# Attention and feed-forward block on one core: the V products moved ahead of the group's piece in TensorE's order

## What is computed

```python
xn = layernorm(x)
# attention branch, 16 heads of 16 features
u, v, q, k = split(silu(xn @ W1 + b1), 4)          # W1: 256 x 1024
scores = einsum("bqhd,bkhd->bhqk", q, k)           # 1024 x 1024 per head
av = einsum("bhqk,bkhd->bqhd", silu(scores) / S, v)
y_attn = layernorm(av * u, gamma, beta) @ W2 + b2
# feed-forward branch, ternary weights, 256 -> 1024 -> 256
h = gelu(layernorm(xn, ln1) @ ternary(w1).T + fb1)
y_ffn = layernorm(h, ln2) @ ternary(w2).T + fb2
out = x + y_attn + y_ffn
```

## Time and profile before

| what | value |
|---|---|
| median of 3 runs | 1671.26 us |
| lowest, highest | 1669.81, 1671.69 us |
| span of the profiled execution | 1672.0 us, first to last instruction; no time beside it is recorded |
| granted TensorE clock, mean | 0.992 of full |
| PE busy | 1575.4 us |
| PEld busy | 762.4 us |
| ACT busy | 1235.2 us |
| DVE busy | 967.6 us |

### The profile page before, as it was taken

The page is one execution under the profiler, slowest core; times in us unless marked ns, Lnnn a source line. Parts: engine busy times, 40 slices in busy tenths (PEclk is TensorE's granted clock), DMA queues, the critical chain, the costliest instruction groups (busy, mean ns, idle before and its releaser), DMA issues.

```text
span 1672.0 us, 27962 instructions
## 1 busy us (share of the span) xinstructions
PE 1575.4 (94%) x9660; PEld 762.4 (46%) x9826; DVE 967.6 (58%) x1844; ACT 1235.2 (74%) x1285; POOL 101.7 (6%) x193
## 2 busy tenths in 40 slices
PE   4799999999999999999999999999999999999997
PEld 3344445444454444444445444544445444454433
DVE  5475645766366563665646655475645756356543
ACT  2477876788668886678767787677876788767884
POOL 2000100001000100001000010000100001000000
PEclk9899999999999999999999999999999999999999
DMA  6470034600445015530345303461034600345000
GB/s 183 97 150 28 1 77 117 135 26 17 89 113 112 26 36 104 120 80 19 75 92 124 67 1 76 92 151 36 1 76 113 141 26 16 84 114 116 1 1 26
DMA packets 110459, 123.68 MB, mean 74 GB/s; under 512 B 6640, under 2 KB 106608, under 8 KB 109296
## 3 DMA queue, kind: packets, MB, share of 16 engines
q1 hardware_dynamic: 110320, 121.81, 32.1%
HBM read 79.84 MB, written 41.94 MB: 73 GB/s over the span
## 4 chain that ended last, share of the span: by engine, by line
PE 70%; ACT 11%; issue 7%; DMA 5%; DVE 3%; SPq 1%; DVEq 0%; ACTq 0%; POOL 0%; POOLq 0%
PE scores L899 22%; PE outs L918 21%; ACT attn L531 9%; PE fill L955 7%; PE fill L989 7%; PE fill L973 5%; DMA QS<-q_scratch 4%; PE fill L982 2%; PE fill L964 2%; PE fill L1005 2%; DMA q_scratch<-qst 1%; PE fill L945 1%; DVE tmp L789 1%; ACT L531 1%; ACT L575 1%
## 5 line engine op out<-in xcount | busy, mean ns | idle before, releaser
L531 ACT ACTIVATE attn<-scores 128x1024 f32<-128x1024 f32 x1024 | 992.2, 1022 | 355.8 <-PE scores L899 353.5
L899 PE MATMUL scores<-QS,KS 128*128 128x512 bf16 x1882 | 514.9, 384 | 62.0 <-issue 28.2
L918 PE MATMUL outs<-attn,V 128*32 128x512 f32 x4096 | 548.7, 608 | 0.4 <-ACT attn L531 0.4
L899 PEld LDWEIGHTS scores<-QS,KS 128*128 128x128 bf16 x2048 | 148.4, 97 | 609.6 <-ACT attn L531 410.1
L789 DVE TENSOR_TENSOR tmp<-fill,l2g 128x512 f32<-128x512 f32 x128 | 88.6, 692 | 147.6 <-PE fill L982 142.0
L918 PEld LDWEIGHTS outs<-attn,V 128*32 128x32 f32 x4096 | 80.8, 108 | 150.4 <-issue 138.3
L989 PE MATMUL fill<-Wq,hgh 128*128 128x256 f32 x512 | 135.6, 303 | 0.3 <-DVE tmp L789 0.2
L955 PE MATMUL fill<-xp,W1h 128*128 128x512 f32 x384 | 132.1, 425 | 3.0 <-DVE xp L813 3.0
L772 DVE SCALAR_TENSOR_TENSOR hid<-fill,ratq,fb1b 128x512 f32<-128x512 f32 x128 | 96.1, 751 | 51.1 <-PE fill L973 39.9
L989 PE MATMUL fill<-Wq,hgl 128*128 128x256 f32 x512 | 125.0, 282 | 0.0
L800 DVE SCALAR_TENSOR_TENSOR part<-fill,cq,part 128x256 f32<-128x256 f32 x64 | 31.0, 484 | 129.6 <-PE fill L989 128.4
(11 more groups left out here) (113 smaller groups left out, 1462.4 us busy)
## 6 DMA issues: line engine op xcount, KB each, us to landing
KS<-k_scratch SPq DMA_DIRECT2D x64, 384.0 KB, 7.1
QS<-q_scratch SPq DMA_DIRECT2D x64, 384.0 KB, 8.3
k_scratch<-kst SPq DMA_DIRECT2D x160, 128.0 KB
q_scratch<-qst SPq DMA_DIRECT2D x96, 128.0 KB
xin<-in_x SPq DMA_DIRECT2D x8, 1024.0 KB, 4.8
KS<-k_scratch SPq DMA_DIRECT2D x32, 256.0 KB, 10.1
QS<-q_scratch SPq DMA_DIRECT2D x32, 256.0 KB, 10.6
out_dram<-part SPq DMA_DIRECT2D x16, 512.0 KB, 2.7
```

The source lines that it names most:

```text
L531: nc.scalar.activation(attn[:, g % 2, 2 * hf:2 * hf + 2, :], SP[:, 2 * hf:2 * hf + 2, :], ACT.Silu).then_inc(s_silu, 1)
L899: ins = mm(SP[:, j, :], KS[:, head, t * P:(t + 1) * P], QS[:, head, h * HALF:(h + 1) * HALF], start=True, stop=True)
L918: ins = mm(OP[32 * j:32 * j + 32, g // RUN % 2, :], V[:, t, c * HPC // 2 + j, o * DH:o * DH + 2 * DH], attn[:, g % 2, j, :], start=(o == 0 ...
```

## The change

In `body` of TensorE the V products of group g-1 move from behind the pieces of group g (and behind the setup products of the first batch) to directly behind the scores of group g. Group 0 and all other engines are as they were.

```diff
                     scores(b, g, first)
                     if g == 0 and not first:
                         times_v(b - 1, GROUPS - 1, False)
+                    if g:
+                        times_v(b, g - 1, first)
                     if first:
                         setup_step(g)
                     for s in steps(g, first, last):
                         step(b, *s)
-                    if g:
-                        times_v(b, g - 1, first)
```

## The result

The changed kernel takes 1713.5 us (median of 4 runs, 1712.6 to 1714.8) against 1671.5 us for the kernel before in the same comparison: ratio 1.0249, 95% interval [1.0236, 1.0263]. The forecast was 1708 us with a range of 1697 to 1724. The profiled span grew from 1672.0 to 1713.0 us, by 41.0 us where the sum said 36.5.

The account below looks back on a forecast made before the run. TensorE's own order was taken to bound groups with a piece. Exposed loads 27.7, gelu.0 5.9 and key and query halves 2.9 us summed to 36.5 us on 1671.3: 1708 us, range 1697 to 1724.

Parts of the forecast that it names:

- the 410 us of "wait for SiLU": Scores' weight loads, 541 waits: of each idle time 0.84 us is the V products running; only what exceeds it is waiting.
- The exposed load: Piece's first load, uncovered behind the V products: 0.093 us in 237 fp32r groups, 0.043 in 132 transpose groups; 27.7 us.
- with nothing lost: Joint from piece to next scores: in group 0 the scores follow the last transpose without loss.
- gelu.0: Group 15: VectorE empties f1.1.1 later, so gelu and group 17's scores come 0.73 us later, 8 times; 5.9 us.
- some 1.3: Predicted sign: a wait for SiLU of some 1.3 us between group 16's piece and group 17's scores.
- The key and query halves: Group 4's scores wait for the DMA restacking q.0.1 of group 61: 0.58 us more, 5 times; 2.9 us.
- pause at the loop's turn: At two of seven batch starts, a pause said to cover group 4's wait for the restacked halves.
- Projections and `xt`: ScalarE's steps for projections and transposed inputs end later but delay nothing that shows; 0 us.
- the rival that all held steps show: ScalarE's held steps cost 0.16 us on each of 96 projections: 15 us more, 1723 us; chance 0.09.
- A hidden load: Rival: the piece's load hides under the V products; only the two uncovered places cost, 11.6 us, 1683 us; chance 0.10.
- Pieces that stop waiting for VectorE: Rival, faster: a piece starting 1 us later finds its input ready; at most 10 us gained, 1662 us; chance 0.04.
- 10 / 369: The faster rival decides only if an exposed load costs less than this, given as 0.026 us.

Follow-up runs that it names:

- the experiment with the fourth score: Against the kernel before, in groups with an fp32r piece: three scores, V products, fourth score, piece; old order elsewhere; 1693.1 us, ratio 1.0120.
- 29 pairs: Kernel before with V products of two neighbouring groups run as one block at 29 places; 1665.5 us, ratio 0.9960; repeated: 1667.4 us, 0.9963.

## Why the prediction was right

**What bounds the kernel.** The reading held that the 410 us of "wait for SiLU" were mostly the V products' own running. The new page shows it: half the wait vanished, its 0.84 us reappeared in front of the pieces, and empty groups didn't change by 0.01 us.

**The exposed load, 27.7 us forecast, 31 measured.** Right in kind, place and sign for both kinds of piece, and the experiment with the fourth score shows the cause. The term was mis-sized for fp32r: 0.093 us forecast, 0.105 measured, 237 times. The difference is the bf16 load of the scores at the piece's other end. The prediction took "with nothing lost" from a row where the scores follow transposes. Behind an fp32r product the scores' load isn't drawn under it, so the bf16 load is exposed after all: 0.105 is close to the full 0.108 of an fp32r load, and the 0.015 that was subtracted isn't saved. The transposes, where the row did apply, came out at 0.046 for 0.043.

**gelu.0, 5.9 us forecast, 6.3 measured.** Right, in all eight batches, and undone by one group's order. Groups 15 and 16 together grew by 0.99 us where 0.92 was forecast. The idle time between group 16's piece and group 17's scores is 1.64 us where "some 1.3" was forecast; about 0.27 of it is the joint behind an fp32r product, as at the end of group 7.

**The key and query halves, 2.9 us forecast, 2.9 left over.** The agreement is luck in the main. Above its own load, group 3 with the wait for these halves grew at all seven starts and not five, by 4.1 us in all. The "pause at the loop's turn" that was to cover it at two of them was TensorE at half its granted clock for a stretch in that one execution. Without the two stretches 3.2 us are gone, one in batch 7 costs 1.5, and the other differences at the starts fill the rest. The chain hangs on `k.0.1` as well as on `q.0.1`; both were moved by the same 1.09 us. How much of the 4.1 us is the change's is uncertain. The first run with 29 pairs has the old order at these starts, and its group 3 grew by 1.2 and 0.7 us in batches 2 and 5 as well, where its clock doesn't fall; at the other starts it differs from before by up to 0.8 us either way.

**Projections and `xt`, 0 forecast.** Right for the projections: 12 in a batch show nothing but their load. For `xt` it was 0.06 us in groups 45 and 57, 0.8 us in all; in the kernel that moves only the fp32r groups, and so not `xt.1`, group 45 is unchanged. ScalarE's held step does delay a SiLU there; the rival that all held steps show is thereby as good as excluded for groups of 2.4 us and longer.

**The rivals.** A hidden load would have left groups with pieces unchanged; they all grew. Pieces that stop waiting for VectorE would have shown as shorter groups at the start of batches or at 42 and 43; apart from group 0 of batches 2 and 5, which is the clock, there is only group 63, and that differs by up to 0.7 us from before in kernels with the old order as well. The bound of that rival, 10 / 369, is 0.027 us and not 0.026, which changes nothing.

The Trainium skill's page "TensorE: Matmul & The Clock Gate", section "Step-by-step: what each phase is for", has loads pulled ahead of running products. The rows of after agree inside the pieces, behind transposes and behind bf16 scores, and disagree at two joints: a full-array load behind V products (0.84 us idle) and a bf16 load behind an fp32r product (0.28 us idle).

## What to carry to other kernels

Before a wait is blamed on the engine that the table names, compare its idle time with the same joint where that engine is long done; if it is the same, it is the own engine's work running, and no reordering removes it. When products of another tile shape must stand in a stream, put the cheapest load (bf16) behind them, and join sets of them where the data allow. A changed order is to be judged over the whole table: with the two orders mixed, a piece and the piece that needs it lost the 1 us between them, which cost more than the change's own term in those groups.

## What the runs showed of the hardware

- A weight load behind four products in 32-column strips is never drawn under them: 0.84 us idle in front of bf16, fp32r and transposes alike, at all 512 such joints of the changed kernel. What it then costs differs: 0.015, 0.108 and 0.058 us from the first load to the second.
- A bf16 load behind an fp32r product of 512 columns starts about 0.23 us after that product's start, together with its own product, while an fp32r load at that place starts with the running product. Behind transposes the bf16 load is drawn under (0.64 us for four loads instead of 0.55, the first ahead of its product).
- Two sets of strip products in a row cost 0.22 us less than two apart. The Trainium skill's page "TensorEngine Tiling (Array Packing)", section "Key Properties", says that a change of tiling mode drains the engine; the 0.22 us for one way in and one way out saved agree in sign, and the page gives no figure.
- VectorE's pause at a loop's turn is 3.05 to 3.75 us in 60 turns, and 5.4 to 6.7 us in the five turns where 384 KB DMAs were issued just ahead of it. Each pause holds one instruction DMA of 8 KB, and VectorE goes on 1.4 to 2.0 us behind its end. TensorE's group 1 waited for it.
- The granted clock of TensorE fell from 2.4 to 1.2 GHz behind idle times of 1.9 to 4.2 us at the starts of batches, and one such stretch cost 1.2 to 1.6 us. It came at some starts and not at others, in two executions of the same kernel too: the first trace of the 29 pairs has none at the turns, its repeat one at the turn into batch 2.
